# Neighbourhood attention inside a four-layer kernel: the product of weights and values with its two sides exchanged

## The reference, cut to what matters

```
q, k, v = split(x @ w_qkv + b_qkv)            # per head, 8 channels
logits  = (q * 8**-0.5) . k + rpb             # the keys of the 7x7 window
out     = softmax(logits) . v
y       = out @ w_proj + b_proj
```

## Time and profile before

| | us |
|---|---|
| median of three runs | 922.51 (922.28 to 922.94) |
| the profiled execution | 920.83 |
| its span | 919.0 |
| PE busy | 693.3 (75% of the span) |
| PE weight loads busy | 423.6 (46%) |
| DVE busy | 739.7 (80%) |
| ACT busy | 536.1 (58%) |
| POOL busy | 422.5 (46%) |
| attention stage | 163.1 to about 323.2 |

### The profile page before, as it was taken

How to read it: one execution, slowest core, us unless ns; L and a number is a source line. 1 busy time by engine, 2 the same in 40 slices (tenths; PEclk the granted TensorE clock), 3 DMA queues, 4 the chain that set the end, 5 groups by cost and what they waited for, 6 DMA issues and landing times.

```text
span 919.0 us, 12627 instructions
## 1 busy us (share of the span) xinstructions
PE 693.3 (75%) x3481; PEld 423.6 (46%) x3481; DVE 739.7 (80%) x977; ACT 536.1 (58%) x668; POOL 422.5 (46%) x237
## 2 busy tenths in 40 slices
PE   4788843899999979415766766767667759499996
PEld 3444421677777743102434444444444624156654
DVE  7999983456555549899999999999999862399997
ACT  1654601455655535946666777777786400299994
POOL 4688852000000031438878889988998800011110
PEclk9999996799999979857789798897997979799999
DMA  2033002540000021110000000000000001100001
GB/s 47 6 92 56 2 1 51 78 80 2 0 0 0 1 71 34 46 36 0 1 1 0 0 0 0 0 0 0 0 1 0 1 1 35 34 1 0 0 0 23
DMA packets 32174, 16.09 MB, mean 18 GB/s; under 512 B 25790, under 2 KB 27582, under 8 KB 32126
## 3 DMA queue, kind: packets, MB, share of 16 engines
q1 hardware_dynamic: 32142, 15.71, 8.8%
HBM read 6.52 MB, written 0.78 MB: 8 GB/s over the span
## 4 chain that ended last, share of the span: by engine, by line
PE 42%; DVE 33%; issue 17%; ACT 4%; POOL 2%; DMA 1%; DVEq 1%; ACTq 0%; SPq 0%; POOLq 0%
PE ps L501 34%; DVE ps L897 8%; DVE arena L1200 7%; DVE arena L897 6%; PE ps L640 4%; DVE arena L949 3%; PE ps L863 3%; ACT ps L1528 1%; DVE ps L949 1%; DVE arena L1128 1%; DVE arena L1155 1%; POOL arena L1569 1%; ACT arena L1531 1%; DMA arena<-arena 0%; PE ps L799 0%
## 5 line engine op out<-in xcount | busy, mean ns | idle before, releaser
L501 PE MATMUL ps<-arena 128*64 128x96 f32 (+7 forms) x1536 | 410.4, 389 | 153.7 <-DVE arena L1200 59.2
L501 PEld LDWEIGHTS ps<-arena 128*64 128x64 f32 (+5 forms) x1536 | 176.4, 139 | 301.0 <-issue 120.7
L1569 POOL TENSOR_TENSOR arena<-arena 128x1024 f32<-128x1024 f32 x91 | 212.7, 2360 | 59.0 <-ACT arena L1536 47.2
L1200 DVE TENSOR_TENSOR_SCAN arena<-arena,ps 128x1024 f32<-128x1024 f32 x72 | 164.6, 2287 | 9.5 <-DVE ps L897 0.5
L1434 ACT ACTIVATE arena<-arena 128x320 f32<-128x320 f32 (+1 forms) x128 | 70.0, 548 | 64.0 <-DVE arena L1086 63.0
L1528 ACT ACTIVATE arena<-arena,a_col 128x1024 f32 (+1 forms) x72 | 82.5, 1145 | 37.6 <-DVE arena L1200 28.5
L897 DVE TENSOR_TENSOR ps<-arena,ps 128x1024 f32<-128x1024 f32 x81 | 98.0, 1209 | 1.4 <-PE ps L501 1.4
L1554 ACT ACTIVATE arena<-ps,nycol 128x1024 f32<-128x1024 f32 x64 | 70.5, 1101 | 46.7 <-PE ps L501 46.7
L1686 POOL TENSOR_TENSOR arena<-arena,bmask 128x128 f32<-128x128 f32 x32 | 14.9, 468 | 153.0 <-PE ps L501 135.2
L1635 POOL MEMSET arena<- 128x6 f32 (+1 forms) x3 | 0.2, 101 | 181.5 <-DVE x2t L1108 181.5
L501 PE MATMUL ps<-ident,arena 128*128 128x128 f32 x384 | 66.3, 331 | 2.9 <-POOL arena L1569 2.9
(11 more groups left out here) (171 smaller groups left out, 1091.2 us busy)
## 6 DMA issues: line engine op xcount, KB each, us to landing
arena<-arena SPq DMA_DIRECT2D x72, 64.0 KB
arena<-arena SPq DMA_DIRECT2D x12, 128.0 KB, 3.8
w_conv<-in_c_far SPq DMA_DIRECT2D x2, 448.0 KB, 7.2
arena<-x SPq DMA_DIRECT2D x12, 64.0 KB, 2.0
arena<-x1t SPq DMA_DIRECT2D x12, 64.0 KB, 2.0
arena<-x3t SPq DMA_DIRECT2D x12, 64.0 KB, 2.0
w_conv<-rpb_pad SPq DMA_DIRECT2D x24, 28.0 KB, 1.8
x<-in_x SPq DMA_DIRECT2D x1, 512.0 KB, 3.7
```

The source lines that it names most:

```text
L501: return pe.matmul(o, l, r, start=start, stop=stop, **k)
L1200: ve.tensor_tensor_scan(hs_ring[n % RING], decay, add, 0.0, ALU.mult, ALU.add).then_inc(S("scan"), 1)
L1569: return gp.tensor_tensor(o, a, b, ALU.mult)
```

## The change

`values` exchanges its sides. The turned exponentials `pt` become stationary (128 keys by 128 or 96 queries), and the moving side is nine columns of `vz`: eight values of one head and a one. The product has queries on its rows, and nine columns per block and head; one PSUM bank (4 or 5, by the image's parity) holds the 288 columns of an image. `vz` is filled once for all images, straight from PSUM. The third key tile is now copied with all 128 queries, so a three-tile copy has 352 columns where it had 320.

`place_values`, `copy_sums`, `ot_b`, the 32 transposes and the one-column copies go. `divide_sums` (DVE) takes reciprocals and quotients straight out of PSUM, for the first three images in step 6 of the next image, for the last after the stage. The loop over images is written out on PE, DVE and ACT. Core of the diff:

```
-                for c, (at, end, q0, q1) in enumerate(seeing(i)):
-                    o = P * (i % 4)
-                    last = mm(ps[0:2 * C, 4 + i // 4, o + q0:o + q1], vz[:, tiles[c], n].rearrange("p a c -> p (a c)"),
-                              pt[:, t % NSB, at:end], start=(n == 0 and i % 4 == 0 and c == 0),
-                              stop=(n == NH - 1 and c == len(tiles) - 1), skip_group_check=True)
+                o = (HD + 1) * (NH * i + n)
+                spans = list(enumerate(seeing(i)))
+                for c, (at, end) in spans[1:] + spans[:1]:
+                    last = mm(ps[0:end - at, 4 + of % 2, o:o + HD + 1], pt[:, u % NSB, at:end],
+                              vz[:, (tiles[c] * B + of) * NH + n], start=(u == 0 and c == 1),
+                              stop=(u == NUNIT - 1 and c == 0), skip_group_check=True)
                 last.then_inc(S("pv"), 1)
...
-            for b in range(B):
-                pe.wait_ge(S("ot_b"), above(b + 1))
-                for i in range(NBLK):
-                    last = pe.transpose(ps[:, b, 2 * C * i:2 * C * i + 2 * C], ot_b[:, b, P * i:P * i + P], ident[0:2 * C, 0:2 * C])
-                last.then_inc(S("sums_turned"), 1)
             pe.wait_ge(S("normalized"), B)
...
             ve.wait_ge(S("v"), 2)
+            ve.wait_ge(S("vz_cleared"), 1)
             for h in range(2):
+                ve.tensor_copy(vz[:, HALF // HD * h:HALF // HD * (h + 1), 0:HD],
+                               ps[:, 6 + h, :].rearrange("p (m d) -> p m d", d=HD)).then_inc(S("v_copied"), 1)
+
+            def divide_sums(b):
+                ve.wait_ge(S("pv"), above(b * NUNIT + NUNIT))
+                v = ps[:, 4 + b % 2, 0:NBLK * NH * (HD + 1)].rearrange("p (i n e) -> p i n e", i=NBLK, n=NH)
+                own(ve.reciprocal(rsum[:, b], v[:, :, :, HD]))
+                own.sync()
+                tt(ot_turned[:, :, b].rearrange("p i (n d) -> p i n d", n=NH), v[:, :, :, 0:HD],
+                   rsum[:, b].unsqueeze(3).to_broadcast([P, NBLK, NH, HD]), ALU.mult).then_inc(S("normalized"), 1)
...
-            with ve.Fori(1, B) as b:
-                attend(b, False)
+            for b in range(B):
+                attend(b)
```

More of the change, by code:

```diff
@@ L78, in seeing @@
     tiles, _, _ = key_tiles(i)
-    spans = [(0, P)] * 2 if len(tiles) == 2 else [(0, P - C), (0, P), (C, P)]
     at, out = 0, []
-    for q0, q1 in spans:
-        out.append((at, at + q1 - q0, q0, q1))
-        at += q1 - q0
+    for rows in [P, P] if len(tiles) == 2 else [P - C, P, P]:
+        out.append((at, at + rows))
+        at += rows
     return out
@@ L92 @@
     "tensor": "sc turned pv b_rep b_share c_rep y_acc crep rowmix prod_turned far_d far_q far_out",
-    "vector": "neg pt_v vz dbu scan nhat prod summed far_off far_pos far_st far_prod",
-    "scalar": "ot_b pexp pt_a c_copied b_copied da y_turned abs hat_y far_hat far_abs",
+    "vector": "neg pt_v dbu scan nhat prod summed far_off far_pos far_st far_prod",
+    "scalar": "pexp pt_a c_copied b_copied da y_turned abs hat_y far_hat far_abs",
     "gpsimd": "hc dbu_sh stat",
@@ L235, in build @@
         k_rows = cv(B * NH, T, dt=BF16, rows=PROD)
-        vt = cv(NBLK, P)
-        vz = cv(NBLK, NH, 2, C)
+        vz = cv(NBLK * B * NH, HD + 1)
         sc = cv(NSB, INNER)
@@ L241, in build @@
         nmax = cv(NSB)
-        ot_b = cv(B, T, rows=2 * C)
         ot = cv(T)
@@ L637, in turn, with attend @@
                 pt_done(b, t - 3 if t % NUNIT >= 3 else t - 2)
-                for c, (_, end, q0, q1) in reversed(list(enumerate(seeing(units[t % NUNIT][1])))):
-                    last = pe.transpose(ps[:, (2, 3, 7)[t % NUNIT % 3], end - q1:end],
-                                        pexp[0:q1, pexp_buffer(t % NUNIT), P * c:P * c + P], ident[0:q1, 0:q1])
+                for c, (at, end) in enumerate(seeing(units[t % NUNIT][1])):
+                    q = end - at
+                    last = pe.transpose(ps[:, (2, 3, 7)[t % NUNIT % 3], at:end],
+                                        pexp[0:q, pexp_buffer(t % NUNIT), P * c:P * c + P], ident[0:q, 0:q])
                 last.then_inc(S("turned"), 1)
             def values(b, t):
-                n, i = units[t % NUNIT]
+                u = t % NUNIT
+                n, i = units[u]
                 tiles, _, _ = key_tiles(i)
-                if t == 0:
-                    pe.wait_ge(S("vz"), above(b + 1))
-                    pe.wait_ge(S("ot_b"), above(b))
+                of = b + t // NUNIT
+                if t == 0 and b >= 2:
+                    pe.wait_ge(S("normalized"), b - 1)
                 pt_done(b, t)
-                for c, (at, end, q0, q1) in enumerate(seeing(i)):
-                    o = P * (i % 4)
-                    last = mm(ps[0:2 * C, 4 + i // 4, o + q0:o + q1], vz[:, tiles[c], n].rearrange("p a c -> p (a c)"),
-                              pt[:, t % NSB, at:end], start=(n == 0 and i % 4 == 0 and c == 0),
-                              stop=(n == NH - 1 and c == len(tiles) - 1), skip_group_check=True)
+                o = (HD + 1) * (NH * i + n)
[4 more added lines that the diff above has]
+                              stop=(u == NUNIT - 1 and c == 0), skip_group_check=True)
                 last.then_inc(S("pv"), 1)
-            def attend(b, first):
-                if first:
+            def attend(b):
+                if b == 0:
                     pe.wait_ge(s_ld["qk0"], QK_LOADS)
@@ L665, in attend @@
                     scores(b, t)
-                    if t >= LAG_TURN or not first:
+                    if t >= LAG_TURN or b:
                         turn(b, t - LAG_TURN)
-                    if t >= LAG_PV or not first:
+                    if t >= LAG_PV or b:
                         values(b, t - LAG_PV)
-            attend(0, True)
-            with pe.Fori(1, B) as b:
-                attend(b, False)
+            for b in range(B):
+                attend(b)
             for t in range(LAG_PV):
@@ L1070, in copy_turned, with attend @@
                 ve.tensor_copy(pt[:, t % NSB, 0:w], ps[:, (2, 3, 7)[t % NUNIT % 3], 0:w]).then_inc(S("pt_v"), 1)
-            def attend(b, first):
+            def attend(b):
                 for t in range(NUNIT):
                     n, i = units[t]
-                    if t == LAG_PV and not first:
-                        place_values(b)
+                    if t == LAG_PV + 2 and b:
+                        divide_sums(b - 1)
                     ve.wait_ge(S("sc"), above(b * NUNIT + (t + 1)))
                     ve.wait_ge(S("pexp"), above(b * NUNIT + (t - NSB + 1)))
-                    if (t - LAG_COPY) % 2 == 0 and (t >= LAG_COPY or not first):
+                    if (t - LAG_COPY) % 2 == 0 and (t >= LAG_COPY or b):
                         copy_turned(b, t - LAG_COPY)
-                    else:
-                        ve.tensor_copy(small[:, 50 + t % 8:51 + t % 8], ident[:, 0:1])
                     tiles, off, (lo, hi) = key_tiles(i)
@@ L1087, in attend @@
                                             1.0, 4 * BIG, ALU.add, ALU.min, nmax[:, t % NSB:t % NSB + 1]).then_inc(S("neg"), 1)
-            place_values(0)
             ve.wait_ge(S("bias_negated"), NH)
-            attend(0, True)
-            with ve.Fori(1, B) as b:
-                attend(b, False)
+            for b in range(B):
+                attend(b)
             for t in range(LAG_COPY):
@@ L1096, in _ @@
                     copy_turned(B, t - LAG_COPY)
[L1098 to L1104, removed]
+            divide_sums(B - 1)
             for h in range(2):
@@ L1417, in copy_turned, with attend @@
                 ac.activation(pt[:, t % NSB, 0:w], ps[:, (2, 3, 7)[t % NUNIT % 3], 0:w], ACT.Copy).then_inc(S("pt_a"), 1)
[L1419 to L1425, removed]
+            def attend(b):
                 for t in range(NUNIT):
                     lo, hi = key_tiles(units[t][1])[2]
-                    if t == LAG_PV and not first:
-                        copy_sums(b - 1)
-                    if (t - LAG_COPY) % 2 and (t >= LAG_COPY or not first):
+                    if (t - LAG_COPY) % 2 and (t >= LAG_COPY or b):
                         copy_turned(b, t - LAG_COPY)
@@ L1436, in _ @@
             ac.wait_ge(S("pexp_cleared"), 1)
-            attend(0, True)
-            with ac.Fori(1, B) as b:
-                attend(b, False)
+            for b in range(B):
+                attend(b)
             for t in range(LAG_COPY):
@@ L1442, in _ @@
                     copy_turned(B, t - LAG_COPY)
-            copy_sums(B - 1)
             for h in range(2):
@@ L1611, in _ @@
             gp.memset(pexp, 0.0).then_inc(S("pexp_cleared"), 1)
[L1612 to L1616, removed]
+            gp.memset(vz, 1.0).then_inc(S("vz_cleared"), 1)
             gp.wait_ge(S("k_hi"), 1)
```

## The result

The changed kernel takes 982.02 us (978.26 to 983.41, 4 runs) against 922.61 us (922.28 to 922.94, 4 runs): ratio 1.0637, 95% interval [1.0606, 1.0669]. The forecast was 982 us, from 950 to 1012. The profiled execution took 978.26 us, its span is 976.5, 57.5 longer than before.

What follows compares the result with a forecast made beforehand. PE was taken to bound the kernel. Stage end +63.5, tail -3.5 and transposes +0.4 us gave +60.4: 981.2 us against the profiled execution, 982.9 against the median; forecast 982, range 950 to 1012.

Steps and rivals of the forecast that it cites:

- The clock stays at 0.50: Attention stage: weight loads do not raise PE's clock, so the whole stage runs at 0.50 (1.2 GHz).
- A load of 128 columns costs 0.21 us at 0.50: Value product's weight loads: 128 columns cost about 0.21 us at clock 0.50, against about 0.11 at 1.00.
- rival B: Attention stage: loads keep their 1.00 pace at clock 0.50, mean step 1.30 us, time 925 us; chance 0.04.
- Steps of 1.86 and 1.32, mean 1.725: Attention stage at 0.50: three-tile step 1.86 us, two-tile 1.32, mean 1.725; 124 steps take 213.9 us.
- the drain of 5.2: End of the attention stage: two turns and four products after the last step take 5.2 us.
- No gaps, first load under the turn: Each step: both gaps at changes of weight shape dropped, product's first load runs beside the last turn.
- rival C: Value product at 0.50: gaps at 96-column weights or first load uncovered, time 1008 us; chance 0.05.
- The tail, 3.5 us: After the last product: turning back starts 1.3 us later instead of 4.8, worth 3.5 us.
- The eight transposes: After the attention stage: they run at 0.50 from the start, costing +0.4 us.
- The start: First four steps of the first image: paced by first exponentials, unchanged, with step 4's scores at 167.38.
- Loop, copies, `vz`, divisions at nothing: Attention stage and before: writing out the loop, larger copies, filling `vz` and two divisions fit idle time, adding nothing.
- Rival A: Attention stage: the clock rises to 1.00, mean step 0.89 us, time 878 us; chance 0.11.

Runs made afterwards that it cites:

- the run with the warm start alone: The changed kernel plus 19 float32 matmuls of 512 columns while PE waits for the query rows and 2 in step 2: 972.89 us.

## Why the prediction was right, point by point

- **The clock stays at 0.50.** Right, and by the mechanism given: under the same loads, 99 moving columns bring the stage to 1.00, while 45 and 9 leave it at 0.50 (889, 988 and 982 us). PE was busy, nearly always with a load under way, for over 99% of the stage in the changed kernel, and that did not raise the clock. Two things in the reasoning were weak. It set 0.92 us of streamed columns in 1.86 beside 4.50 and 5.30 us of *busy* time in 6.60, which holds the way through the array as well. And it took the stage's own pattern to fix the clock, while two kernels with the same steady stage lie 101 us apart by their start alone; the forecast held because this stage does start at 0.50.
- **A load of 128 columns costs 0.21 us at 0.50.** Right: the mean step was 1.71 us, where rival B, in which loads keep their pace, had 1.30. The Trainium skill ("TensorE: Matmul & The Clock Gate", section "LDWEIGHTS (loading the stationary operand)") gives a load as its columns over 1.2, with no clock in it; for 64 columns more that is 53 ns, an estimate from the page. The traces agree with it at 1.00 (192 against 136 ns, 56 more) and not at 0.50 (326 against 220 ns, 106 more).
- **Steps of 1.86 and 1.32, mean 1.725.** Step 4 of the first image starts at 165.9 and the last loads end at 382.96. Less the drain of 5.2 this leaves 211.9 us for 124 steps, 1.71 each. The steady steps repeat within 0.01 us of 1.84, 1.79, 1.68 and 1.52, two of each in eight, since turns and products of different units meet in a step; their mean is the same 1.71. No steady step is a pure two-tile step of 1.32, so only the mean was forecast well. The term was 2 us too large.
- **No gaps, first load under the turn.** Right, rival C is out. That the gaps came with the change between 64 and 128 weight columns was argued then, and the runs with 128 and 96 wide weights bear it out.
- **The tail, 3.5 us.** Measured 3.2 (4.8 - 1.6). The eight transposes took 1.97 instead of 1.33 us, so +0.6 where the forecast had +0.4.
- **The start.** I let it stand; in the profiled execution step 4 came at 165.9, not 167.4. Nearly all of these 1.5 us lie ahead of the first scores (161.69, before 163.14). The runs with 99 and 45 moving columns, the same kernel up to there, have them at 163.44 and 163.10, so this shift differs from one execution to the next and is not the change.
- **The sum.** -1.5 (start) - 2.2 (steps) + 0.2 (drain) + 0.3 (tail) + 0.3 (transposes and what follows) = -2.9 against +60.4: +57.5, as the spans of the profiled executions show. The medians moved by 59.4. That the median of 982.02 met the forecast of 982 to a hundredth is luck; the working as a whole was off by 1 to 3 us in 60.
- **Loop, copies, `vz`, divisions at nothing.** Writing out the loop: shown. The others were not tried alone. Inside the stage DVE has 88.5 us of work in 217 us, so they have room. DVE and ACT were busy for 41% and 42% of it, where I had said under 40%.
- **Rival A, 878 us.** The clock's rise didn't come by itself; with it forced and held, 886 and 888 us. Its step of 0.89 us was somewhat small: in the run with the warm start alone, eight steps at 1.00 took 7.45 us (171.46 to 178.91), 0.93 each. The clock held only with extra streaming; with the warm start alone it fell 17 us into the stage.

The exchange is worth having once the stage runs at 1.00: 886 against 922 us. The kernel before gets some 26 of these 36 us (2.9%) by 96 weight columns alone.

## What to carry to other kernels

Before a rewrite that turns moving columns into weight loads, look at what the stage streams at 1.2 GHz, and not only at how long PE is busy. Here PE was busy all the time, and the rewrite still took away the clock at which it would have paid, which doubled the price of its loads. Look at the start of the stage too. This stage could not raise the clock by itself; 21 float32 matmuls in idle time before it and in its step 2, with one cheap bf16 matmul per unit beside the float32 loads, were worth 96 us (982.02 to 886.25). The 21 alone left the kernel at 972.89 us, and the bf16 matmuls alone (two in a three-tile unit) at 989.40. Before making weights smaller or larger, look at the shape on either side: in this kernel 64 weight columns among 128 cost 0.09 us at each change, and 96 among 128 cost none.

## What the runs showed that was not expected

- A stage can have two lasting paces with the same instructions: 989.40 and 888.23 us, decided in its first microseconds.
- With two matmuls less, a kernel took 97 us more (886.25 to 983.34).
- The idle time at a change between 64 and 128 weight columns, 0.09 us at 1.00 and 0.14 at 0.50, and the first load that it leaves uncovered made up 26 us of the kernel before. Weights widened for rows that nobody reads took them away.
